# Weight casts and small loads moved earlier in a state-space and mixture-of-experts layer on eight cores

## What is computed

```python
xn = layernorm(x)
# state-space branch
z = xn @ W_in                          # 1024 -> 4112: x, B, C, dt
xs = silu(conv1d_4taps(z.x))           # 2048 channels = 16 heads x 128
y = scan(h = a_t*h + xs_t (x) B_t;  y_t = h . C_t)     # 16 heads, state 64
y = sigmoid(xn @ W_gate) * y
y = y * rsqrt(mean(y*y) + eps) * norm_w
attn = y @ W_out                       # 2048 -> 1024
# experts: all 8 are computed for every token, one is kept
route = softmax(xn @ router_w);  best = argmax(route)
for e in range(8):
    a, g = split(xn @ w1[e])           # 1024 -> 2 x 4096
    out = where(best == e, (silu(a)*g) @ w2[e], out)   # 4096 -> 1024
return x + attn + out * max(route)
```

## Time and profile before

| | us |
|---|---|
| the two timed runs | 8885.76 and 9272.86 |
| their median | 9079.31 |
| the profiled execution | 8276.93 |
| its span on the slowest core (2) | 8275.4 |
| spans of the eight cores | 8248.9 to 8275.4 |
| PE busy with matmuls | 6569.8 (79% of the span) |
| DVE busy | 3249.8 (39%) |
| ACT busy | 1677.6 (20%) |

### The profile page before, as it was taken

How to read it: one execution, slowest core, us unless ns; L and a number is a source line. 1 busy time by engine, 2 the same in 40 slices (tenths; PEclk the granted TensorE clock), 3 DMA queues, 4 the chain that set the end, 5 groups by cost and what they waited for, 6 DMA issues and landing times.

```text
span 8275.4 us, 90986 instructions; the slowest of 8 cores (8248.9 to 8275.4 us)
## 1 busy us (share of the span) xinstructions
PE 6569.8 (79%) x28776; PEld 2842.0 (34%) x28776; DVE 3249.8 (39%) x6770; ACT 1677.6 (20%) x1615; POOL 65.8 (1%) x130
## 2 busy tenths in 40 slices
PE   4545459899898989899844454599998989899897
PEld 1112124344343434444311121244443434344343
DVE  3443533433334343433334435333333343433333
ACT  1313212122121312112022032121121312122130
POOL 0000000000000000000000000000000000000000
PEclk9568579999999999999985685799999999999998
DMA  4114024434444444444441140244344444434343
GB/s 129 47 38 145 1 77 138 140 127 153 126 154 128 140 141 133 147 133 148 126 139 34 42 141 1 87 133 148 125 155 124 157 129 138 143 126 155 125 155 110
DMA packets 408969, 979.76 MB, mean 118 GB/s; under 512 B 47584, under 2 KB 310016, under 8 KB 338880
## 3 DMA queue, kind: packets, MB, share of 16 engines
q1 hardware_dynamic: 400896, 956.48, 35.6%
q0 software_dynamic: 7616, 17.46, 0.7%
HBM read 965.10 MB, written 8.39 MB: 118 GB/s over the span
## 4 chain that ended last, share of the span: by engine, by line
PE 72%; DVE 12%; issue 6%; DMA 5%; ACT 3%; DVEq 2%; ACTq 1%; POOL 0%; SPq 0%; POOLq 0%
PE p_fo L1230 21%; PE p_fa L1127 20%; PE p_fg L1137 20%; DVE acc L1284 2%; DVE tmp L1280 2%; PE p_w L922 2%; PE p_sb L633 2%; DMA stg<-w1t 1%; PE p_z L411 1%; PE p_z L335 1%; DMA stg<-wgate 1%; ACT L667 1%; DMA stgw<-w2t 1%; PE pY L795 1%; PE p_cv L358 1%
## 5 line engine op out<-in xcount | busy, mean ns | idle before, releaser
L1230 PE MATMUL p_fo<-A,w2bf 128*128 128x512 bf16 x8192 | 1877.4, 393 | 412.3 <-DVE w2bf L1192 412.3
L1127 PE MATMUL p_fa<-xn,wbf 128*128 128x512 bf16 x8192 | 1855.5, 380 | 29.7 <-DVE wbf L1112 24.8
L1137 PE MATMUL p_fg<-xn,wbf 128*128 128x512 bf16 x8192 | 1851.6, 379 | 0.0
L1149 ACT ACT_TABLE_LOAD x512 | 656.9, 1283 | 4397.4 <-PE p_fa L1127 4397.4
L1082 DVE TENSOR_TENSOR A<-wbf,p_fg 128x1024 bf16<-128x1024 bf16 x512 | 625.0, 1221 | 2144.9 <-PE p_fg L1137 2144.9
L1230 PEld LDWEIGHTS p_fo<-A,w2bf 128*128 128x128 bf16 x8192 | 821.2, 101 | 1466.1 <-issue 568.5
L1127 PEld LDWEIGHTS p_fa<-xn,wbf 128*128 128x128 bf16 x8192 | 800.4, 98 | 1005.1 <-issue 46.9
L1137 PEld LDWEIGHTS p_fg<-xn,wbf 128*128 128x128 bf16 x8192 | 801.6, 98 | 966.5
L1192 DVE CAST w2bf<-stgw 128x256 bf16<-128x256 f32 x2048 | 587.7, 293 | 1187.7 <-PE p_fo L1230 916.7
L1112 DVE CAST wbf<-stg 128x2048 bf16<-128x2048 f32 x484 | 593.8, 1227 | 51.6 <-DVE A L1082 2.7
L1149 ACT ACTIVATE wbf<-p_fa 128x1024 bf16<-128x1024 f32 x512 | 524.4, 1024 | 5.7
(11 more groups left out here) (145 smaller groups left out, 2485.2 us busy)
## 6 DMA issues: line engine op xcount, KB each, us to landing
stg<-w1t SPq DMA_DIRECT2D x512, 1024.0 KB, 4.8
stgw<-w2t SPq DMA_DIRECT2D x2048, 128.0 KB, 2.2
stg<-win_x SPq DMA_DIRECT2D x64, 768.0 KB, 4.4
stg<-wgate SPq DMA_DIRECT2D x64, 512.0 KB, 4.4
stg<-wout SPq DMA_DIRECT2D x32, 1024.0 KB, 4.9
stg<-win_b SPq DMA_DIRECT2D x32, 512.0 KB, 3.6
stg<-win_c SPq DMA_DIRECT2D x32, 512.0 KB, 3.4
acc<-u_t POOLq DMA_DIRECT2D x16, 512.0 KB, 12.1
```

The lines of the kernel that those rows point to most:

```text
L1127: ins = t.matmul(p_fa[p][:, tsl * 512:(tsl + 1) * 512], wbf[:, p * 2048 + k * 128: p * 2048 + (k + 1) * 128], xn[:, k * HT + tsl * 512: k ...
L1137: ins = t.matmul(p_fg[p][:, tsl * 512:(tsl + 1) * 512], wbf[:, p * 2048 + 1024 + k * 128: p * 2048 + 1024 + (k + 1) * 128], xn[:, k * HT + ...
L1149: ins = s.activation(wbf[:, p * 2048: p * 2048 + 1024], p_fa[p][:, :], AF.Silu)
L1230: ins = t.matmul(p_fo[gp_par * 4 + o2 * 2 + tsl][:, :], w2bf[:, s4 * 256 + o2 * 128: s4 * 256 + (o2 + 1) * 128], A1[:, j * HT + tsl * 512: ...
```

## The change

It has four parts.

1. `rowbuf` grows from 512 to 2048 elements. One POOL load per chunk `kq` brings all 16 rows; the four `p_sb` matmuls read a quarter each. 64 loads become 16.
2. The loads and casts of the first two output-weight blocks are written at the end of `ssd_phase`, ahead of its barrier, and `rms_wout_phase` begins with them done.
3. `router_phase` no longer asks for two PSUM tiles that it did not use.
4. In `ffn_phase` the first four w2 loads and casts of the next group are written ahead of `f_v2` for every group, and at `og == 2` ahead of the w1 loads and casts as well.

```diff
-        rowbuf = sb("rowbuf", [1, 512], F32)
+        rowbuf = sb("rowbuf", [1, 2048], F32)
...
+                state["gate_mm_last"] = g_mm[-1]
                 barrier()
...
                 for kq in range(QT // Q):
                     pe_sb, sb_ve, sb_ac = [], [], []
                     mp_hist = []
+
+                    def f_g(g, kq=kq, prev_pe_sb=prev_pe_sb):
+                        g.wait_ge(sems["ve"], ve_d2)
+                        g.wait_ge(sems["pe"], prev_pe_sb)
+                        inc(g.dma_start(
+                            out=rowbuf[0:1, :],
+                            in_=nsc_hm[kq * 16:(kq + 1) * 16, :]), "dG", 16)
+                    sect("gpsimd", f_g)
+                    dg_f = C["dG"]
                     for qq in range(4):
-                        def f_g(g, kq=kq, qq=qq, prev_pe_sb=prev_pe_sb):
-                            g.wait_ge(sems["ve"], ve_d2)
-                            if qq >= 1:
-                                g.wait_ge(sems["pe"], pe_sb[qq - 1])
-                            else:
-                                g.wait_ge(sems["pe"], prev_pe_sb)
-                            inc(g.dma_start(
-                                out=rowbuf[0:1, 0:512],
-                                in_=nsc_hm[kq * 16 + qq * 4: kq * 16 + (qq + 1) * 4, :]),
-                                "dG", 16)
-                        sect("gpsimd", f_g)
-                        dg_f = C["dG"]
...
                             ins = t.matmul(p_sb[:, :], onesrow[:, :],
-                                           rowbuf[0:1, 0:512],
+                                           rowbuf[0:1, qq * 512:(qq + 1) * 512],
                                            start=True, stop=True)
...
                 state["ssd_prev_ac"] = C["ac"]
+                wo_pd, wo_pc = [], []
+                for o in range(2):
+                    def f_qw(g, o=o):
+                        g.wait_ge(sems[state["stg_cast_last"][0]],
+                                  state["stg_cast_last"][1])
+                        ins = g.dma_start(out=stg[:, o * 2048:(o + 1) * 2048],
+                                          in_=wout[o, :, :])
+                        wo_pd.append(inc(ins, f"dW{o}", 16))
+                    sect("sync", f_qw)
+
+                    def f_cw(v, o=o, gml=state["gate_mm_last"]):
+                        v.wait_ge(sems[f"dW{o}"], wo_pd[o])
+                        v.wait_ge(sems["pe"], gml)
+                        ins = v.tensor_copy(wbf[:, o * 2048:(o + 1) * 2048],
+                                            stg[:, o * 2048:(o + 1) * 2048])
+                        wo_pc.append(inc(ins, "ve"))
+                    sect("vector", f_cw)
+                state["wo_pref"] = (wo_pd, wo_pc)
                 barrier()
...
                 for o in range(NKC):
                     p = o % 2
+                    if o >= len(wo_dma):
...
-                  pt("p_st1", [8, 128], F32) as p_st1,
-                  pt("p_sb", [128, 512], F32) as p_sb,
-                  pt("p_sb2", [128, 512], F32) as p_sb2):
+                  pt("p_st1", [8, 128], F32) as p_st1):
...
+                        elif og > 0 and state.get("w2_pend_next"):
+                            w2_dma = list(state["w2_pend_next"][0])
+                            w2_cast = list(state["w2_pend_next"][1])
+                            state["w2_pend_next"] = None
...
-                        if og == 3 and e < NE - 1:
+                        nxt = None
+                        if og < 3:
+                            nxt = (e, og + 1)
+                        elif e < NE - 1:
+                            nxt = (e + 1, 0)
+                        if nxt is not None:
                             n_dma, n_cast = [], []
                             for jn in range(4):
-                                emit_w2_dc(jn, e + 1, 0, n_dma, n_cast,
+                                emit_w2_dc(jn, nxt[0], nxt[1], n_dma, n_cast,
                                            w2_cast[28 + jn], w2_mm[28 + jn])
-                            state["w2_pend"] = (n_dma, n_cast)
+                            if og < 3:
+                                state["w2_pend_next"] = (n_dma, n_cast)
+                            else:
+                                state["w2_pend"] = (n_dma, n_cast)
```

More of the change, by code:

```diff
@@ L890, in rms_wout_phase @@
                 sect("vector", f_v3)
-                wo_dma, wo_cast, wo_mm, wo_ev = [], [], [], []
+                pref = state.get("wo_pref")
+                if pref is not None:
+                    wo_dma, wo_cast = list(pref[0]), list(pref[1])
+                    state["wo_pref"] = None
+                else:
+                    wo_dma, wo_cast = [], []
+                wo_mm, wo_ev = [], []
                 for o in range(NKC):
                     p = o % 2
[L896 to L913, removed]
@@ new lines, in rms_wout_phase, with f_q, f_c @@
+                    if o >= len(wo_dma):
+                        def f_q(g, o=o, p=p):
+                            if o >= 2:
+                                g.wait_ge(sems["ve"], wo_cast[o - 2])
+                            else:
+                                g.wait_ge(sems[state["stg_cast_last"][0]],
+                                          state["stg_cast_last"][1])
+                            ins = g.dma_start(out=stg[:, p * 2048:(p + 1) * 2048],
+                                              in_=wout[o, :, :])
+                            wo_dma.append(inc(ins, f"dW{p}", 16))
+                        sect("sync", f_q)
+                        def f_c(v, o=o, p=p):
+                            v.wait_ge(sems[f"dW{p}"], wo_dma[o])
+                            if o >= 2:
+                                v.wait_ge(sems["pe"], wo_mm[o - 2])
+                            ins = v.tensor_copy(wbf[:, p * 2048:(p + 1) * 2048],
+                                                stg[:, p * 2048:(p + 1) * 2048])
+                            wo_cast.append(inc(ins, "ve"))
+                        sect("vector", f_c)
@@ L1202, in ffn_phase @@
                             elif j < 4:
-                                if og == 0:
-                                    emit_w2_dc(j, e, og, w2_dma, w2_cast,
-                                               state["prev_w2_cast"],
-                                               state["prev_ffn_mm"])
-                                else:
-                                    emit_w2_dc(j, e, og, w2_dma, w2_cast,
-                                               prev_cast[28 + j],
-                                               prev_mmlist[28 + j])
+                                emit_w2_dc(j, e, og, w2_dma, w2_cast,
+                                           state["prev_w2_cast"],
+                                           state["prev_ffn_mm"] if og == 0 else None)
                             else:
```

2 lines of the change are left out of this document (1 added, 1 removed).

## The result

The changed kernel is faster: the ratio of its time to that of the kernel before is 0.9741, with a 95% interval of 0.9699 to 0.9783. The forecast was 0.9856, within 2% of no change. In many timed executions of either kernel TensorE's clock was held lower on one die or both, which is why the median of 9079 us stood so far above the profiled 8277; the comparison leaves those out. The lowest times over all runs of this study are 8105.92 us for the changed kernel and 8265.47 for the kernel before.

A forecast was written before the change was run, and what follows sets the result against it. The expert phase was taken as bound by PE, with PE's stops to be won. 109 + 0 + 11 - 1 = 119 us saved gave 8158 us profiled, ratio 0.9856, 8949 us timed; range 0.973 to 1.000, or 8060 to 9140 us.

The forecast's parts named there:

- the long boundaries: 14 expert group ends with w1 loads: stop as long as before, gain 0; bounds 48 us won, 69 us lost.
- the output weights: Start of the output-weight phase, 4 times: 2.8 us gained each from casting two blocks earlier, 11 us together.
- the row loads: Router row loads: 48 fewer, only four waited for, each growing to 8 KB; 1 us lost, bounds -3 to +3.
- PE stops for 3.9 us instead of 7.15.: 34 short expert group ends without w1 loads: stop moves from block 0 to block 4, 3.2 us less each, 109 us.
- I take the full 2.6 us, unchanged from before, so no gain from it.: Half clock after the short-boundary stops: still costs 2.6 us each, no gain; bounds 0 to 2.6 us.
- all-or-nothing rival: Short boundaries: clock stays up over the 3.9 us stop, 88 us more, 207 saved, ratio 0.975; chance 0.14.
- bound of 12.1 us for the slowest landing: Long boundaries: w1 loads landing in 12.1 us, 4.9 us later than before, would lose 69 us over 14 boundaries.
- waits near 302 us: Sign in the profile: PE's waits for w2 casts fall from 412.3 to about 302 us, still about 50 of them.

The follow-up runs named there:

- e4: Part 4 of the change alone, against the kernel before, with the old order kept at the 14 group ends with w1 loads; mean span 8110 us.
- e8: Part 1 alone (one row load per chunk in place of four), against the kernel before; single time 8284.26 us, mean span 8253.5 us.
- e3: Parts 1 to 3 of the change without part 4, against the kernel before; mean span 8235 us.
- e1_again: The changed kernel, unchanged, profiled and timed again; profiled span 8104.3 us, ratio 0.9788 to the kernel before.
- e2: Part 4 alone (w2 casts ahead of the eviction), against the kernel before; mean span 8105 us, ratio 0.9854.
- e9: The changed kernel plus four products that nobody reads behind the eviction of groups 0 to 2; mean span 8264 us.
- e10: The changed kernel with all four eviction pairs (groups 0 to 2) and the w1 casts moved behind casts of the next group; lowest time 7909.13 us.
- e12: The kernel of e11 with the w1 loads cut into eight 256 KB pieces spread between w2 loads, w1 casts later; lowest time 7897.53 us.
- e11: The kernel of e10 with each output-weight cast ahead of the addition of the block two before it; lowest time 7761.0 us.

## Why the prediction was off

Its mechanism held: the stop moved to block 4 and was halved, the long boundaries did not get worse, the output weights gave a little, the row loads nothing. Its size did not: 119 us were forecast, and 8263 - 8088 = 175 us were found by the mean spans of the two profiles, 158 by the averages over more executions.

- **"PE stops for 3.9 us instead of 7.15."** It is 3.58 at most boundaries and 3.6 on average (the terms of the forecast, added without rounding, give 4.0). I had let the last cast end before the eviction, 0.29 us, where the row shows the next instruction 0.21 us after the cast's start, and took more for the restart than it needs. 34 x 0.3 = 10 us.
- **"I take the full 2.6 us, unchanged from before, so no gain from it."** This is the step that failed most. 2.6 was one restart; the mean of the 34 before was 2.4 us. And it fell, to 1.7 (1.5 and 1.8 in groups 1 and 2, 2.6 in the two short ones in group 3), since about one stop in four of this length leaves the clock at 2.4 GHz. 34 x 0.7 = 24 us. The rows that said so were there: after equal stops of 2.62 us blocks of 3.61 and 5.02 us. On the six cores with complete records of the kernel before, 90 of the 144 blocks behind such a stop (the third to the eighth of a phase) last 3.6 us and 54 last 4.9 us or more: half clock behind 38%. I read the two rows as "even 2.6 can do it" and gave the other reading a chance of 0.14 as an all-or-nothing rival. It was neither: the price rises with the length of the stop, and the table above has the points between.
- **Long boundaries, "gain 0".** The stops are 10.96 us on average before and 9.95 after, 14 x 1.0 = 14 us between these two profiles. But it isn't shown to come from the change: with the old order in place e4 has 10.3 us, e8 10.65, and cores 0, 1 and 3 of e3 have 10.2, and single cores of the kernel before lie between 10.2 and 11.9. The landings above tell the same: in e3 the loads land as soon as after the change. The forecast of 0 stands within what can be told. (Its bound of 12.1 us for the slowest landing was a median; the slowest single one, of `acc`, took 18.7 us.)
- **Output weights, 11 us.** 21 - 10 = 11: right, and e3 shows both halves.
- **Row loads, -1 us.** Right within what can be told (e8).

10 + 24 + 14 = 48 us, and between the two profiles the expert phases gave 155 where 109 was forecast: 46 more. The 10 us that remain between 119 + 46 and 175 lie in phases that the change doesn't touch and within what cores scatter. By the averages over more executions 158 - 119 = 39 us were missed, and the first two terms, 34 us, are nearly all of it.

The averages give a ratio of 8095/8253 = 0.981; the lowest times give 8105.92/8265.47 = 0.981; e1_again, timed again, gave 0.9788 with 0.9711 to 0.9866. The first ratio, 0.9741, sets 8114.05 and 8127.80 us against 8333.57 and 8340.21 for the kernel before, and these two are 62 us and more above what that kernel took in six later executions; why isn't on record. So the change is worth about 2%, probably less than the first ratio says; on which side of 2% it lies stays open. The forecast had one slip of its own as well: 207 us saved is a ratio of 0.975, not the 0.973 that it gives as the end of its range.

The check that I had listed, waits near 302 us, shows the shorter stops: they are 268 us. The half clock behind them it can't show.

## What to carry over

A stop of TensorE costs its length and then the half clock behind it, and the second part is not a yes or no: here, in groups 1 and 2, it was on average 0.1 us or less after 0.6 us, 0.3 to 0.8 us after 2.1, 1.5 to 1.8 after 3.6 and 2.2 to 2.5 from 6.7 on. In group 3 it was 2.2 after 3.2 us already, so take such a curve from the place that you are about to change, and count over all its stops and cores before you price one. Before a work item is moved ahead of another in an in-order queue, look whether the other could be cut up instead: with two of the eviction's four pairs placed between later casts (e6) the expert phases took 196 us less than with the eviction whole. A small load behind a large one in the same queue waited for it here: DVE stood 5.28 us. And compare one profile with one profile only after looking how far executions of one kernel lie apart: up to 16 us in mean span for the kernel before and 21 for the changed one, more than the smaller terms of this forecast.

## What was unexpected

The clock was granted neither in full nor by half in some stretches, but at 0.81. In the profiled executions of e1, e2, e6 and e9, as in that of the kernel before, no core has such a stretch. In e10 to e12, which have the fewest stops, they add up to 163 us (e10, least) to 2144 us (e11, most) of a core's time. I don't take it as shown that fewer stops bring them on: e8, which stops as often as the kernel before, has 140 us of them on two cores, e3 and e4 have over 2500 us on four, and in its execution of 7761.00 us e11 had a mean granted clock of 0.90 on all eight cores.
